# Two fused graph attention layers on one core: seeds of the next chunk of rows written before the chunk changes, and its conversions, row maxima and epilogue waits moved to later steps

## The chip, the core and the metric

The program runs on 1 core of a Trainium2 chip. The metric is the device time of one execution in microseconds (us). Three runs of the kernel before took 660.51, 660.71 and 661.35 us; their median is 660.71 us. The profiled execution took 661.77 us, of which the profile's span covers 660.0 us.

Engines in the profile: PE is TensorE (PEld its weight loads), DVE is VectorE, ACT is ScalarE, POOL is GpSimd, SP is SyncE, which here only issues DMAs.

## The reference

Two layers work on `x` (4096 nodes, 64 features) and one adjacency matrix `adj` (4096 x 4096, int32, symmetric, about 0.2% ones). Each is masked softmax attention, a residual and a layer norm:

```
Wh = item_embs @ W;  We = entity_embs @ W
scores = (Wh @ a1)[:, None] + (We @ a2)[None, :]
e = where(scores > 0, scores, 0.2 * scores);  e = where(adj > 0, e, NEG_BIG)
h = softmax(e, axis=1) @ entity_embs + item_embs
x = layernorm(x + elu(h))                       # layer 0
wh = x @ weight_w
e = leaky_relu((wh @ a_src)[:, None] + (wh @ a_dst)[None, :], 0.01)
x = layernorm(x + softmax(where(adj > 0, e, -1e9), axis=1) @ wh + bias)   # layer 1
```

## The kernel before, in words

**Chunks and steps.** The 4096 output rows are 32 row tiles of 128. They are worked through in chunks of 4, 8, 8, 8 and 4 tiles (`WIDTHS`), twice: chunks C0 to C4 are layer 0, C5 to C9 layer 1. A chunk goes through 32 steps J = 0..31, one for each tile of 128 columns of `adj`. The step number over the whole program is k = 32C + J, so C2 begins with step 64 and C7 with step 224. One step does this:

- PE multiplies the mask tile `v` with a diagonal matrix `D` of the chunk (L986) into one of three PSUM buffers `zps` (`ZB = 3`). This writes, or adds, the mask's term of the scores.
- The term of the leaky ReLU comes in one of two ways. In an unseeded step DVE adds it after the matmul (L816, `SCALAR_TENSOR_TENSOR`, for short the STT). In a seeded step ACT has written it ahead (L605, a Relu of `S_row`, the seed) and the matmul adds on top of it, so DVE has nothing to do.
- ACT takes the exponential into `Pm` (L613), in every step.
- PE multiplies `Pm` with the features (L941) and in layer 0 with ones (L948), two steps later (`LAG = 2`).

`SEEDS` says how many steps of each chunk are seeded. A seed of step n is issued on ACT one or two steps before n, ahead of the exponential of that step (`seeds_at`). It has to wait for its buffer: the user three places before it in the list `users` must be done. Before the change, only steps whose buffer was last used by a step of the same chunk may be seeded (`may`).

**What is done beside the steps.** While chunk C runs, the next chunk is prepared. In layer 0 the int32 `adj` halves of its tiles are converted to `v`: by DVE (L701, `compare`) or, for the tiles in `ACT_TILES` (4, 6, 8, 10, 20 and 24), by ACT (L506, `convert`). `halves_at` gives the step. C3 has the tiles 20 to 27, so the first tile that is converted during C2 is one of ACT's. In both layers DVE takes maxima over each row tile in two pieces (L722, `row_max`; `pieces_at` gives the step), which in layer 0 read the converted tile. At J = 30 DVE makes the next chunk's `D` (L733 to L744, `diagonals`). PE cannot begin the next chunk before that (`D_ready`).

**The epilogue of the chunk that ended** runs on POOL during the next chunk (L398 to L435), with parts elsewhere at fixed steps: ACT saves the sums at J = 1 (L543) and the projected rows at J = 4 (L560, L565), PE projects at J = 3 (L915, L920), DVE takes reciprocals at J = 7 (L441) and reduces `sums`, `squares` and (layer 0) `scores` at the steps of `AFTER_WIDE`, `AFTER_LAST` (C4) and `IN_LAYER_1`; in layer 0 the new row scores are turned on PE at J = `rows` and saved by ACT one step later (L516, L517).

**Order.** There is no scheduler: every engine executes its program in the order in which the loops over C and J write it, and waits on semaphores where named. Within a step DVE's order is: reductions of the epilogue, STT, conversions, row maxima, at J = 30 the diagonals. ACT's is: parts of the epilogue, conversions, seeds, exponential. On SP's queue a chunk's loads of `adj` come first, then the stores of the rows that ACT saved (L332, L334), then the load of `S_row` for the next chunk but one in the buffer of the same parity (L326).

## Time and profile before

| | |
|---|---|
| median of 3 runs | 660.71 us |
| profiled execution | 661.77 us |
| span of the profile | 660.0 us |
| DVE busy | 575.0 us, 87% of the span |
| ACT busy | 516.2 us, 78% |
| PE busy | 515.8 us, 78% |
| POOL busy | 191.6 us, 29% |
| TensorE clock granted, mean | 0.954 of 2.4 GHz |

A chunk is best read from the end of its `D` on DVE to the end of the next chunk's `D`, since between these two DVE does one chunk's whole work and PE runs one chunk's steps. The ends lie at 107.1, 179.9, 254.4 and 318.7 us (for C1 to C4) and at 390.5, 436.2, 496.3, 559.8 and 615.9 us (for C5 to C9). A busy share near the length of such a stretch says that the engine could not have done the chunk in much less. The gap between C4's last step and C5 (about 26 us) is the serial passage from layer 0 to layer 1.

### The profile page before, as it was taken

The numbers are of one execution on the slowest core, as the hardware profiler recorded it, in microseconds if no ns is written. First come the engines' busy times: TensorE is split into PE (matmuls) and PEld (weight loads), VectorE is DVE, ScalarE is ACT, GpSimd is POOL, SyncE is SP. The second block draws the span as 40 slices with busy tenths as digits, with TensorE's granted clock in tenths as the row PEclk, the third lists the DMA queues.
The fourth block names the chain that finished last, engine by engine and source line by source line (L and its number), as shares of the span: only waits on it lengthen the run. The fifth ranks groups of instructions, "written<-read, shape, count | busy, mean of one in ns | idle before, by whom it ended". The sixth has DMA issues, their size and how long they took to land.

```text
span 660.0 us, 14220 instructions
## 1 busy us (share of the span) xinstructions
PE 515.8 (78%) x6038; PEld 230.8 (35%) x6039; DVE 575.0 (87%) x729; ACT 516.2 (78%) x592; POOL 191.6 (29%) x143
## 2 busy tenths in 40 slices
PE   1304779899989799999988318778897898899894
PEld 1202345343443344444454203233333233333341
DVE  3888998999999898888467889989998998899685
ACT  0855998899999996898676227979997899699673
POOL 0110000388028850672083000004311450232240
PEclk9999889899999899999998758999999999999998
DMA  7899885687478727430200000000000001000000
GB/s 165 319 360 334 280 285 210 241 288 257 180 242 291 250 94 287 132 126 2 73 3 18 1 32 1 1 33 1 2 9 33 1 1 33 1 1 18 1 17 9
DMA packets 18631, 76.46 MB, mean 116 GB/s; under 512 B 6552, under 2 KB 8776, under 8 KB 10376
## 3 DMA queue, kind: packets, MB, share of 16 engines
q1 hardware_dynamic: 17560, 74.63, 32.5%
q8 instruction: 47, 0.77, 0.5%
q0 software_dynamic: 256, 0.80, 0.4%
...
HBM read 74.47 MB, written 1.09 MB: 114 GB/s over the span
## 4 chain that ended last, share of the span: by engine, by line
PE 31%; DVE 25%; ACT 20%; issue 14%; DMA 4%; POOL 3%; SPq 1%; POOLq 0%; ACTq 0%; DVEq 0%
PE acc L941 16%; ACT Pm L613 14%; DVE junk L722 12%; PE zps L986 9%; DVE zps L816 8%; PE acc L948 4%; DMA adj_in<-in_adj 4%; ACT zps L605 2%; ACT v L506 2%; SPq L350 1%; DVE v L701 1%; DVE tAB L697 1%; ACT u_row L522 1%; DVE tot L757 0%; DVE tot L753 0%
## 5 line engine op out<-in xcount | busy, mean ns | idle before, releaser
L613 ACT ACTIVATE Pm<-zps,ebias 128x1024 f32<-128x1024 f32 (+1 forms) x320 | 293.4, 933 | 82.6 <-DVE zps L816 68.3
L722 DVE CUSTOM_DVE_ANT_0 junk<-v,u_row 128x2048 int8<-128x2048 int8 (+3 forms) x136 | 304.6, 2261 | 2.0 <-ACT v L506 1.8
L986 PE MATMUL zps<-D,v 128*128 128x128 bf16 x2048 | 173.7, 224 | 56.1 <-DVE D L744 29.1
L986 PEld LDWEIGHTS zps<-D,v 128*128 128x128 fp8e4 x2048 | 118.7, 99 | 216.3 <-issue 87.3
L816 DVE SCALAR_TENSOR_TENSOR zps<-S_row,tau_col,zps 128x1024 f32<-128x1024 f32 (+1 forms) x136 | 142.0, 1050 | 50.6 <-PE zps L986 47.7
L605 ACT ACTIVATE zps<-S_row,ntau_col 128x1024 f32<-128x1024 f32 (+1 forms) x184 | 176.6, 960 | 5.4
L941 PE MATMUL acc<-Pm,X 128*32 128x512 f32 (+1 forms) x1280 | 145.5, 527 | 20.2 <-ACT Pm L613 17.8
L941 PE MATMUL acc<-Pm,VE 128*32 128x512 f32 (+1 forms) x1280 | 148.6, 538 | 8.5 <-ACT Pm L613 3.9
L398 POOL TENSOR_TENSOR tAB<-flag,totW 128x520 f32<-128x520 f32 (+1 forms) x8 | 10.3, 1287 | 282.5 <-issue 138.7
L948 PE MATMUL acc<-Pm,ones 128*32 128x256 f32 (+1 forms) x1280 | 87.8, 347 | 0.0
L948 PEld LDWEIGHTS acc<-Pm,ones 128*32 128x32 f32 x1280 | 43.1, 115 | 72.2 <-issue 62.7
L701 DVE TENSOR_SCALAR v<-adj_in 128x2048 fp8e4<-128x2048 int32 x44 | 62.7, 1428 | 1.0 <-DMA adj_in<-in_adj 1.0
L506 ACT ACTIVATE v<-adj_in,tanh_bias 128x2048 fp8e4<-128x2048 int32 x20 | 39.7, 2003 | 7.9 <-DMA adj_in<-in_adj 7.9
L941 PEld LDWEIGHTS acc<-Pm,X 128*32 128x32 f32 x1280 | 25.4, 108 | 42.4 <-ACT Pm L613 29.7
L941 PEld LDWEIGHTS acc<-Pm,VE 128*32 128x32 f32 x1280 | 25.8, 110 | 28.1 <-ACT Pm L613 11.6
L466 POOL TENSOR_SCALAR var<-tot 128x8 f32<-128x8 f32 (+1 forms) x10 | 7.7, 773 | 64.6 <-DVE tot L757 64.6
L405 POOL TENSOR_TENSOR o<-o,rden 128x512 f32<-128x512 f32 (+1 forms) x8 | 13.2, 1644 | 27.4 <-DVE rden L441 27.4
L401 POOL TENSOR_TENSOR o<-o,tAB 128x520 f32<-128x520 f32 (+1 forms) x8 | 13.5, 1687 | 25.8 <-ACT o L560 14.7
L467 POOL TENSOR_TENSOR rstd<-var,mhalf 128x8 f32<-128x8 f32 (+1 forms) x10 | 18.1, 1809 | 0.8
L887 PE MATMUL acc<-identf,ext 128*2 128x128 f32 (+2 forms) x3 | 1.1, 374 | 21.3 <-DVE ext L659 21.3
L506 ACT ACT_TABLE_LOAD x1 | 1.3, 1283 | 19.1 <-DMA adj_in<-in_adj 19.1
L425 POOL TENSOR_SCALAR mean<-tot 128x8 f32<-128x8 f32 (+1 forms) x8 | 6.4, 804 | 30.3 <-DVE tot L753 30.3
...
## 6 DMA issues: line engine op xcount, KB each, us to landing
...
```

Of the source, the lines that this page charges most:

```text
L401: ns.tensor_tensor(o[:, 0:n, :], o[:, 0:n, :], tA[:, 0:n, :], ALU.add).then_inc(flag_added, 1)
L405: link(ns.tensor_tensor(h, h, per_row(rden[:, 0:n]), ALU.mult))
L467: g.tensor_tensor(rstd[:, 0:R(C)], var[:, 0:R(C)], mhalf[:, 0:R(C)], ALU.pow).then_inc(rstd_done, 1)
L506: a.activation(v[:, H // 2, H % 2 * HALF:(H % 2 + 1) * HALF], adj_in[:, H % AB, :], ACT.Tanh, bias=tanh_bias[:, :], scale=40.0, saturate=F ...
L605: a.activation(zps[:, buf("step", n), 0:R(C) * P], S_row[:, C % 2, 0:R(C) * P], ACT.Relu, bias=ntau_col[:, n % JT:n % JT + 1]).then_inc(se ...
L613: a.activation(Pm[:, k % PB, 0:R(C) * P], zps[:, buf("step", k), 0:R(C) * P], ACT.Exp, bias=ebias[:, int(seeded(k)), J:J + 1])\
L701: d.tensor_scalar(v[:, H // 2, H % 2 * HALF:(H % 2 + 1) * HALF], adj_in[:, H % AB, :], 0.0, 0.5, ALU.is_gt, ALU.subtract, saturate=False). ...
L722: d.tensor_tensor_reduce(out=junk[:, at % 2, 0:cols.stop - cols.start], in0=v_bytes[:, rt, cols], in1=u_row[:, cols], scale=1.0, scalar=-3 ...
L816: d.scalar_tensor_tensor(z, S_row[:, C % 2, 0:R(C) * P], tau_col[:, J:J + 1], z, ALU.max, ALU.add).then_inc(z_done, 1)
L941: last = t.matmul(acc[s * F + f:s * F + f + G, 0, 0:w], V[:, f:f + G], Pm[:, k % PB, s * w:(s + 1) * w], start=first, stop=end)
L948: last = t.matmul(acc[q * G:(q + 1) * G, 1, 0:w], ones[:, :], Pm[:, k % PB, q * w:(q + 1) * w], start=first, stop=end)
L986: last = t.matmul(zps[:, buf("step", k), r * P:(r + 1) * P], v[:, chunks[C][1] + r, J * P:(J + 1) * P], D[:, C % 2, r, :], start=(r * P % ...
```

## The change

Four things change.

1. The rule of which steps may be seeded is widened: the buffer's last user may be a step of the chunk before, in the same layer, if that chunk is at least as wide. ACT then writes the seed for the next chunk at J = 30 and first waits until `S_row` of that chunk has landed (`wait_S`). The counts in `SEEDS` stay. Seeded steps per chunk were 28, 27, 27, 16, 12 and 28, 18, 18, 10, 0; they are 28, 27, 28, 16, 12 and the same in layer 1.
2. The seeded steps are spread by another formula, which takes the first candidate instead of the last. C2, C3, C4, C7 and C8 now begin with a seeded step 0; C1 and C6 begin with steps 0, 1 and 2 unseeded, as before. C0 and C5 keep their pattern.
3. `CLEAR = 3`: in every chunk except C0, the conversions for the next chunk begin at J = 3 instead of J = 0 and the row maxima at J = 4 instead of J = 1. Their last steps stay (25 and 28), so they stand closer.
4. The steps at which DVE, PE and ACT do their parts of POOL's epilogue are 1 to 2 later (`elu` 11 to 12, `sums` 14 to 16, `squares` 18 to 20, `scores` 24 to 26, `rows` 26 to 28; in layer 1 14 to 16 and 19 to 21). `AFTER_LAST` (C4) stays.

```diff
-    AFTER_WIDE = dict(elu=11, sums=14, squares=18, scores=24, rows=26)
+
+    CLEAR = 3
+    AFTER_WIDE = dict(elu=12, sums=16, squares=20, scores=26, rows=28)
     AFTER_LAST = dict(elu=10, sums=13, squares=17, scores=21, rows=22)
-    IN_LAYER_1 = dict(sums=14, squares=19)
+    IN_LAYER_1 = dict(sums=16, squares=21)
...
             may = [k for k in range(JT * C, JT * (C + 1)) if place["step", k] >= ZB
-                   and users[place["step", k] - ZB][0] == "step" and users[place["step", k] - ZB][1] >= JT * C]
+                   and users[place["step", k] - ZB][0] == "step"
+                   and users[place["step", k] - ZB][1] >= JT * FIRSTS[layer(C)]
+                   and R(users[place["step", k] - ZB][1] // JT) >= R(C)]
             n = SEEDS[layer(C)][C - FIRSTS[layer(C)]]
-            seeded_steps |= {k for i, k in enumerate(may) if (i + 1) * n // len(may) > i * n // len(may)}
+            seeded_steps |= {k for i, k in enumerate(may) if i * n % len(may) < n}
...
-            return [h for h in range(first, end) if (h - first) * 27 // (end - first) == J]
+            clear = CLEAR if C else 0
+            return [h for h in range(first, end) if clear + (h - first) * (27 - clear) // (end - first) == J]
...
-            return [(i, i // 2, i % 2) for i in range(n) if i * 29 // n + 1 == J]
+            clear = CLEAR if C else 0
+            return [(i, i // 2, i % 2) for i in range(n) if clear + i * (29 - clear) // n + 1 == J]
...
                     for n in seeds_at.get(k, []):
+                        of = n // JT
+                        if of > C:
+                            wait_S(act, of)
                         wait_buf(act, "step", n)
-                        a.activation(zps[:, buf("step", n), 0:R(C) * P], S_row[:, C % 2, 0:R(C) * P], ACT.Relu,
+                        a.activation(zps[:, buf("step", n), 0:R(of) * P], S_row[:, of % 2, 0:R(of) * P], ACT.Relu,
                                      bias=ntau_col[:, n % JT:n % JT + 1]).then_inc(seed_done, 1)
```

The lines move by 7 to 10 in the changed kernel (L816 is L826 there, L722 is L732, L613 is L623, L605 is L615, L506 is L513).

DVE at the start of C2, from the last operation of C1 on (`D` is C2's, the STTs are steps of C2, `junk,um` is a row maximum for C3). Before:

```order
L744 TENSOR_SCALAR D<-identb,g 128x128 x8
L816 SCALAR_TENSOR_TENSOR zps<-S_row,tau_col,zps 128x1024 x2
L722 ISA junk,um<-v,u_row 128x2048
L722 ISA um 128x1
L816 SCALAR_TENSOR_TENSOR zps<-S_row,tau_col,zps 128x1024
L722 ISA junk,um<-v,u_row 128x2048
```

and after the change:

```order
L754 TENSOR_SCALAR D<-identb,g 128x128 x8
L826 SCALAR_TENSOR_TENSOR zps<-S_row,tau_col,zps 128x1024
L732 ISA junk,um<-v,u_row 128x2048
L732 ISA um 128x1
L826 SCALAR_TENSOR_TENSOR zps<-S_row,tau_col,zps 128x1024
```

Before, the STTs are those of steps 64, 65 and 66 and the first row maximum belongs to J = 1. After, the STTs are those of steps 65 (J = 1) and 69 (J = 5) and the first row maximum belongs to J = 4.

ACT over the change from C1 to C2, from the saved rows of the epilogue (L517, after the change L524) or the last seeds of C1 to the second conversion for C3. Before:

```order
L605 ACTIVATE zps<-S_row,ntau_col 128x1024
L613 ACTIVATE Pm<-zps,ebias 128x1024 x3
L506 ACTIVATE v<-adj_in,tanh_bias 128x2048
L613 ACTIVATE Pm<-zps,ebias 128x1024
L543 ACTIVATE tAB<-acc 128x512
L548 ACTIVATE tAB<-acc 128x256
L506 ACTIVATE v<-adj_in,tanh_bias 128x2048
```

and after the change:

```order
L524 ACTIVATE rowsS<-zps 4x128
L615 ACTIVATE zps<-S_row,ntau_col 128x1024
L623 ACTIVATE Pm<-zps,ebias 128x1024
L615 ACTIVATE zps<-S_row,ntau_col 128x1024
L623 ACTIVATE Pm<-zps,ebias 128x1024 x2
L615 ACTIVATE zps<-S_row,ntau_col 128x1024
L623 ACTIVATE Pm<-zps,ebias 128x1024
L550 ACTIVATE tAB<-acc 128x512
L555 ACTIVATE tAB<-acc 128x256
L623 ACTIVATE Pm<-zps,ebias 128x1024
L615 ACTIVATE zps<-S_row,ntau_col 128x1024
L623 ACTIVATE Pm<-zps,ebias 128x1024
```

The row that follows the last one shown is the first conversion for C3 (L513). The second seed after the saved rows is that of step 64, the next one that of step 66. The conversion was the work ahead of the first exponential of C2 and now stands behind the third.

DVE at the start of C7. Before:

```order
L744 TENSOR_SCALAR D<-identb,g 128x128 x8
L816 SCALAR_TENSOR_TENSOR zps<-S_row,tau_col,zps 128x1024 x2
L722 ISA junk,um<-v,u_row 128x2048
L722 ISA um 128x1
L816 SCALAR_TENSOR_TENSOR zps<-S_row,tau_col,zps 128x1024
```

and after the change:

```order
L754 TENSOR_SCALAR D<-identb,g 128x128 x8
L826 SCALAR_TENSOR_TENSOR zps<-S_row,tau_col,zps 128x1024 x2
L732 ISA junk,um<-v,u_row 128x2048
L732 ISA um 128x1
L826 SCALAR_TENSOR_TENSOR zps<-S_row,tau_col,zps 128x1024
```

The rows read alike, but the first two STTs were those of steps 224 and 225 (J = 0 and 1) and are now those of steps 225 and 227 (J = 1 and 3).

## Rows read from the trace of the kernel before

**Rows 1.** Windows, `D` to `D`: length; PE, PEld, DVE, ACT, POOL busy; clock; DMA.

```profile
107.10:179.90 72.80, 67.00 (x808) 29.85 (x801) 69.33 (x76) 66.52 (x71) 34.02 (x17) 0.98 0.63 220
179.90:254.40 74.50, 67.67 (x786) 29.73 (x782) 70.37 (x71) 72.59 (x72) 41.43 (x17) 0.98 0.67 233
254.40:318.70 64.30, 63.59 (x769) 28.52 (x762) 54.71 (x58) 52.76 (x56) 27.91 (x17) 1.00 0.36 123
390.50:436.20 45.70, 32.79 (x363) 13.14 (x364) 44.61 (x53) 37.73 (x60) 0.00 (x0) 0.89 0.01 1
436.20:496.30 60.10, 51.54 (x528) 20.13 (x525) 56.87 (x64) 54.17 (x55) 15.01 (x11) 1.00 0.04 14
496.30:559.80 63.50, 53.71 (x524) 20.74 (x520) 59.79 (x65) 54.38 (x54) 18.59 (x11) 0.97 0.04 13
559.80:615.90 56.10, 51.55 (x524) 20.38 (x520) 49.11 (x53) 47.33 (x47) 14.21 (x11) 1.00 0.03 9
```

**Rows 2.** Page, part 5: the exponentials; busy, mean ns, idle before and releaser.

```profile
L613 ACT ACTIVATE Pm<-zps,ebias 128x1024 f32<-128x1024 f32 (+1 forms) x320 | 293.4, 933 | 82.6 <-DVE zps L816 68.3
```

**Rows 3.** Timeline, DVE, start of C2: start us, us, operation, idle before.

```profile
180.98 1.29 DVE L816 SCALAR_TENSOR_TENSOR zps<-S_row,tau_col,zps 128x1024 f32<-128x1024 f32 x1 [1.09 <-PE zps L986]
182.88 1.29 DVE L816 SCALAR_TENSOR_TENSOR zps<-S_row,tau_col,zps 128x1024 f32<-128x1024 f32 x1 [0.61 <-PE zps L986]
184.08 2.28 DVE L722 CUSTOM_DVE_ANT_0 junk<-v,u_row 128x2048 int8<-128x2048 int8 x1
```

**Rows 4.** Timeline, ACT, start of C2.

```profile
182.30 1.11 ACT L613 ACTIVATE Pm<-zps,ebias 128x1024 f32<-128x1024 f32 x1
184.33 0.60 ACT L543 ACTIVATE tAB<-acc 128x512 f32<-128x512 f32 x1 [0.92 <-PE acc L948]
...
185.09 2.00 ACT L506 ACTIVATE v<-adj_in,tanh_bias 128x2048 fp8e4<-128x2048 int32 x1
...
188.13 1.12 ACT L605 ACTIVATE zps<-S_row,ntau_col 128x1024 f32<-128x1024 f32 x1
```

**Rows 5.** Timeline, ACT and SP, saved rows and load of `S_row` in C1.

```profile
171.37 0.25 ACT L517 ACTIVATE rowsS<-zps 4x128 f32<-4x128 f32 x1
...
172.39 0.35 SPq L326 DMA_DIRECT2D S_row<-S_rows_scratch  x1
```

**Rows 6.** The landing of that load of `S_row` (L326).

```profile
DMA to landing us min/median/max: 5.2/5.2/5.2
```

**Rows 7.** Timeline, DVE, start of C7.

```profile
497.32 1.29 DVE L816 SCALAR_TENSOR_TENSOR zps<-S_row,tau_col,zps 128x1024 f32<-128x1024 f32 x1 [1.02 <-PE zps L986]
...
499.99 2.28 DVE L722 CUSTOM_DVE_ANT_0 junk<-v,u_row 128x2048 int8<-128x2048 int8 x1
```

**Rows 8.** Timeline, PE, start of C7: the projection and step 227.

```profile
501.46 1.16 PE L915 MATMUL zps<-W1p,tAB 128*128 128x130 f32 x8
502.46 0.61 PE L986 MATMUL zps<-D,v 128*128 128x128 bf16 x8
```

**Rows 9.** Timeline, DVE, start of C6.

```profile
440.33 2.29 DVE L722 CUSTOM_DVE_ANT_0 junk<-v,u_row 128x2048 int8<-128x2048 int8 x1
```

**Rows 10.** Timeline, ACT, start of C6: step 194.

```profile
443.86 1.11 ACT L613 ACTIVATE Pm<-zps,ebias 128x1024 f32<-128x1024 f32 x1 [2.07 <-DVE zps L816]
```

**Rows 11.** Timeline, DVE, start of C5.

```profile
392.65 3.79 DVE L697 TENSOR_REDUCE tAB<-X 128x64 f32<-128x2048 f32 x1
...
400.77 0.75 DVE L816 SCALAR_TENSOR_TENSOR zps<-S_row,tau_col,zps 128x512 f32<-128x512 f32 x1
```

**Rows 12.** Timeline, ACT, start of C8: steps 261 and 262.

```profile
574.74 2.12 ACT L613 ACTIVATE Pm<-zps,ebias 128x1024 f32<-128x1024 f32 x2 [2.79 <-DVE zps L816]
```

**Rows 13.** Groups by form, DVE, C2: row maxima, busy and mean ns.

```profile
L722 DVE CUSTOM_DVE_ANT_0 junk<-v,u_row 128x2048 int8<-128x2048 int8 x16 | 41.0, 2564 | 0.0
```

**Rows 14.** Timeline, POOL, C9: last operation of C8's epilogue.

```profile
639.26 1.04 POOL L430 TENSOR_TENSOR tAB<-tAB,rstd 128x512 f32<-128x512 f32 x1
```

**Rows 15.** Timeline, ACT, end of C9: the sums are saved.

```profile
649.93 0.38 ACT L543 ACTIVATE tAB<-acc 128x256 f32<-128x256 f32 x1 [0.76 <-PE acc L941]
```

## The prediction, made before the changed kernel ran

> **What bounds the kernel now.** I read the windows from the end of one `D` to the end of the next first. In five of the seven chunks shown DVE is busy for nearly the whole length: 69.33 of 72.80 us in C1, 70.37 of 74.50 in C2, 44.61 of 45.70 in C5, 56.87 of 60.10 in C6, 59.79 of 63.50 in C7 [rows 1]. So DVE idles 3.5, 4.1, 1.1, 3.2 and 3.7 us there, 15.6 us in all. ACT is as full in C2 (72.59 of 74.50) and has 6 to 9 us of idle time in C1, C5, C6 and C7. In C3 PE is the full one, 63.59 of 64.30 us. Only C8 leaves every engine room (PE 51.55, DVE 49.11, ACT 47.33 of 56.10). The page's groups then say that the exponentials are waited for: ACT sat idle 82.6 us ahead of them, 68.3 us of it until an STT of DVE came [rows 2]. That reads like a chance for this change, since many of these waits lie in a chunk's first steps. But an idle ACT beside a full DVE gives nothing back: to shorten such a chunk, DVE must do less or wait less. So the question for each part is what DVE does between one `D` and the next.
>
> **What the change does to DVE's work.** A seed takes one STT (1.29 us [rows 3]) from DVE and gives ACT a Relu (1.12 us [rows 4]). The counts stay, except that C2 gets one seed more. So DVE saves 1.3 us in the whole kernel, and seeds across the boundary only move the other STTs to later steps of the same chunk. The row maxima and conversions keep their number too, and so does POOL's epilogue. What changes is when DVE may do them. Because every engine runs in program order, the STTs of J = 0 to 3 now stand in front of the first row maximum, and DVE has nothing to put into the waits between them. `CLEAR` takes away the cover.
>
> **C2.** `D` ends at 179.9 us, which I call 0. Before, DVE waits 1.1 and 0.6 us, does two STTs and starts the first row maximum at 4.2 [rows 3]; 2.4 us of its idle time lies later. After, that first maximum reads tile 20, which ACT converts at J = 3. ACT gets there like this: the sums of C1 are saved at 4.4 as before (they wait for PE's last products of C1) and take 0.9 with the second copy; then exponential 65, seed 67, exponential 66 at 1.1 each and the conversion at 2.0 [rows 4]. That is 10.7 at the earliest. It can be later by the new wait for `S_row`: rows saved until 171.6, load issued at 172.4, landed 5.2 us behind that [rows 5, 6], so 6.0 us from saved to landed, of which ACT fills 2.2 with a seed and an exponential. The 3.8 us left are partly hidden, since DVE still has two maxima, an STT and `D` to do after the scores that this depends on (2 x 2.28 + 1.29 + 3.0 = 8.9 us), but exponentials 62, 63 and seed 66 then still stand ahead of exponential 64; worked through, that makes the first maximum up to 1.9 later, 12.6. I take 11.5. DVE does one STT until then, so it idles 10.2, and 1.5 more ahead of step 69, whose buffer waits for rows that ACT saves after that conversion. Of the 2.4 us of later idle time I leave 0.6, as the reductions come two steps later and wait less for POOL. Sum: 70.4 - 1.3 + 10.2 + 1.5 + 0.6 = 81.4 against 74.5: **+6.9 us**. Bounds: 10.7 and no other wait, +4.0; 12.6 with all waits, +9.8.
>
> **C7.** `D` ends at 496.3. DVE's first maximum now follows the STT of step 227. PE reaches that step only after the projection, 502.46 + 0.61 [rows 8], and nothing in the change makes the projection earlier, since it waits for the saved sums. So the STT runs from 6.8 to 8.1, and DVE has done two STTs, 2.5 us of work, by then. Before, it had idled 1.2 us by that time and done 6.9 [rows 7]. Loss 4.4. DVE's other idle time in C7 is 2.5 us, from STTs for which it came early; now it comes late, and I let 1.1 of it vanish: **+3.3** (bounds 1.9 and 4.4).
>
> **C6.** Steps 192 to 194 are unseeded before and after, then 196 is. Before, one row maximum lay between the second and third STT, from 440.33 [rows 9], and one more behind it. After, STT 194 ends at 441.6, exponential 194 at about 444.0 (two exponentials and a seed of 1.1 each behind 440.7; before it began at 443.86 [rows 10]), and step 196, which takes that buffer, has its STT until 446.5. By then DVE is two maxima behind and one STT ahead, 4.6 - 1.3 = 3.3. It can recover part of 1.4 us: **+2.5** (2.1 to 3.3).
>
> **C5.** DVE sums the columns until 396.4, then did two maxima and STT 164 at 400.77 [rows 11]. Now STT 164 comes first. PE was held by the column totals too and needs three small steps, ACT a copy, until about 399.0. DVE waits 2.6 us, and it was full otherwise: **+2.6** (1.8 to 3.1).
>
> **C1.** Three STTs run back to back, then a conversion; then STT 37 waits for saved rows: **+1.0** (-0.6 to 2.0).
>
> **C8.** Here DVE has 7.0 us idle, so a smoother start counts. Exponential 261 began at 574.74, 14.9 behind `D`, after a wait of 2.79 us [rows 12]. Without maxima between the STTs I get 12.0. That is 2.9 us, of which a maximum that is still to be done takes some: **-2.0** (-4.0 to 1.0).
>
> **At nothing.** C3: PE is full and idles 0.7 us [rows 1]; DVE's later start is hidden by its 9.6 idle us (-0.7 to 1.5). C0 keeps its order. C4 is tied to POOL's chain, whose steps stay. C9: C8's epilogue ends on POOL at 640.3 [rows 14]; two steps of 0.9 us later is 642.1, and ACT needs the stored result only at 649.93 [rows 15].
>
> **The sum.** 1.0 + 6.9 + 2.6 + 2.5 + 3.3 - 2.0 = 14.3 us on the execution profiled, 661.8 to 676.1; on the median of 660.7 that is **675.0 us**. The bounds add up to +4.5 and +25.1.
>
> **GpSimd's port.** Row maxima alone take 2.28 us [rows 3]; the 16 of C2, where POOL is busy 41.4 of 74.5 us, take 2.56 on the mean [rows 13, 1]. Of the maxima, two in each of C1, C2, C6 and C7 move from steps ahead of POOL's epilogue into it. At 0.28 each that is 2.2 us, which I leave to the range, as POOL meets DVE no longer than before. The Trainium skill (SBUF — State Buffer, "Who interferes with whom") says that a DVE instruction with two SBUF inputs and a GpSimd instruction exclude each other: the second fully blocks until the first is through. The trace's mean of 0.28 us is far from that for the maxima.
>
> **Rivals.**
> - *VectorE catches up* (668 us). The losses at the starts are real, but the idle time inside the chunks is used up by them in full, C2's first maximum comes at 10.7, C8 gives 4: about +7. For it: 2.5 us in C7 and 2.4 in C2 are there. Against it: C5 has none.
> - *The wait for `S_row` is in the open* (681 us). At each of three boundaries (C1 to C4) up to 3.8 us of ACT; half of that on top of the sum, +6. ACT is full in C2, which speaks for it; DVE's rest of 8.9 us against it.
> - *The maxima collide with GpSimd* (693 us). If each of the eight moved ones were held up by its own length, 8 x 2.28 = 18 us more. The mean in C2 speaks against it.
> - *Faster: the starts were the bound* (651 us). ACT waits behind row maxima at the starts (2.07 us in C6 [rows 10], 2.79 in C8 [rows 12]). If the STTs, free of them, came so soon that DVE waited under 1 us at a start, it would start its maxima no later than before and chunks could shrink by DVE's idle time, 15.6 us in five of them and some 5 in C8. Half of that is -10. It decides at the first maximum of C2: it would have to start before 5 us behind `D`. The conversion on ACT in front of it speaks against that.
> - *Nothing moves* (660.7 us): gains at C8 and C3 cancel the rest.
>
> **Numbers.** Forecast 0.50, catching up 0.22, `S_row` 0.10, GpSimd 0.04, faster 0.09, nothing 0.05. Within 0.2% (1.3 us) is what a measurement of this kernel cannot tell from no change. Slower by more than that 0.86, within it 0.05, faster 0.09. The range of 8 in 10 leaves out the faster case, nothing and the collision: 665 to 683 us.
>
> **What would show it.** Right: the windows of C2, C5, C6 and C7 are longer by 7, 3, 2.5 and 3 us with DVE's busy time unchanged; DVE's idle time sits ahead of the STTs and the first maximum of each chunk, and in C2 ends with ACT's conversion; ACT and PE wait for DVE late in the chunks. C3 stays at 64 us, C8 is shorter. Wrong: first maxima at 5 us behind `D` or sooner, or chunks whose DVE busy time fell by more than an STT.

## The result: 682.3 us, slower by 3.2%

The changed kernel takes 682.25 us (median of 4, 681.46 to 682.68) against 661.03 for the kernel before (median of 4): ratio 1.0315, 95% interval 1.0294 to 1.0337, so +21.2 us. The forecast was 675.0 in a range of 665 to 683. Sign and range hold, the range by less than 1 us, and the number is 7 us short. The execution profiled took 682.1 us, its span 680.3 (before: 661.8 and 660.0). The engines' busy times, part 1 of the page of the changed kernel:

```profile
PE 519.7 (76%) x6039; PEld 231.3 (34%) x6039; DVE 573.1 (84%) x728; ACT 518.3 (76%) x593; POOL 181.3 (27%) x143
```

In the kernel before DVE was busy 575.0 us, so it now works 1.9 us less while the span is 20.3 us longer. ACT is busy 2.1 us longer, 1.1 of it for one seed more, and PE 3.9 us longer with one matmul more on record (6039 for 6038). On DVE, the engine that the forecast watched, all of the loss is waiting. Part 5 of the page names the groups that wait (busy, mean ns of one, then idle time before the group and what ended most of it); first the kernel before, then the changed one:

```profile
L722 DVE CUSTOM_DVE_ANT_0 junk<-v,u_row 128x2048 int8<-128x2048 int8 (+3 forms) x136 | 304.6, 2261 | 2.0 <-ACT v L506 1.8
L816 DVE SCALAR_TENSOR_TENSOR zps<-S_row,tau_col,zps 128x1024 f32<-128x1024 f32 (+1 forms) x136 | 142.0, 1050 | 50.6 <-PE zps L986 47.7
```

```profile
L732 DVE CUSTOM_DVE_ANT_0 junk<-v,u_row 128x2048 int8<-128x2048 int8 (+3 forms) x136 | 305.2, 2269 | 8.0 <-ACT v L513 7.9
L826 DVE SCALAR_TENSOR_TENSOR zps<-S_row,tau_col,zps 128x1024 f32<-128x1024 f32 (+1 forms) x135 | 140.3, 1048 | 70.5 <-PE zps L996 67.7
```

DVE waits 70.5 us ahead of its STTs, up from 50.6, and 8.0 ahead of the row maxima, up from 2.0: 25.9 us more between them, on the engine that was full in five of the seven chunks of [rows 1]. Where it lies shows in the windows from `D` to `D` of the changed kernel, C1 to C3 and C5 to C8, columns as in [rows 1]:

```profile
107.90:184.00 76.10, 67.77 (x804) 29.99 (x796) 69.82 (x75) 67.26 (x71) 28.75 (x17) 0.96 0.60 211
184.00:265.70 81.70, 68.50 (x782) 29.70 (x782) 69.17 (x70) 73.84 (x74) 32.48 (x17) 0.98 0.61 213
265.70:333.20 67.50, 65.36 (x782) 29.17 (x782) 54.51 (x59) 51.83 (x55) 30.58 (x17) 1.00 0.33 110
403.20:452.90 49.70, 33.33 (x372) 13.29 (x372) 44.64 (x52) 39.26 (x62) 0.00 (x0) 0.90 0.04 12
452.90:515.90 63.00, 52.85 (x516) 20.61 (x516) 57.60 (x65) 54.78 (x54) 10.40 (x11) 0.97 0.03 11
515.90:578.90 63.00, 52.41 (x520) 20.37 (x520) 57.29 (x64) 54.96 (x54) 20.34 (x11) 1.00 0.03 10
578.90:635.60 56.70, 52.73 (x520) 20.75 (x520) 48.53 (x52) 44.72 (x44) 15.19 (x11) 0.97 0.02 6
```

Length less DVE's busy time is what it idles. In C2 that is 12.5 us, where it was 4.1, and in C1 6.3 (3.5), C3 13.0 (9.6), C5 5.1 (1.1), C6 5.4 (3.2), C7 5.7 (3.7), C8 8.2 (7.0).

Below stands every kernel that ran, by chunk: how much longer (us) each chunk is, from the end of one `D` to the end of the next, than in the profiled execution of the kernel before. "Median" is the difference of the medians of timed executions on one chip. The last column runs from C9's `D` to the end. The chunks come from one execution each. How far they scatter can be seen where a kernel's order in a chunk is that of the kernel before: C0 and what precedes it by about 1 us, C1 by up to 0.9 (only_spread, across_c7), C4 by up to 1.2 (more_seeds, across_c7), C2, C3 and C5 to C9 by 0.3 at most.

```
                median     C1    C2    C3    C4    C5    C6    C7    C8    C9
forecast         +14.3   +1.0  +6.9   0     0    +2.6  +2.5  +3.3  -2.0   0
after            +21.2   +3.4  +7.3  +3.1  -1.9  +4.2  +2.8  -0.5  +0.6  +0.6
no_clear         +11.8   +0.9  +2.6  +3.4  -1.9   0.0  +3.0  -1.3  +3.1  +0.6
only_clear       +13.2   +1.8  +5.9  -0.4  -0.2  +4.2  +1.7  -0.4  +1.3   0.0
clear_max        +16.7   +1.7  +5.3  +1.3  -1.2  +4.2  +1.6  -0.4  +1.2  -0.1
only_seeds        +5.7   -0.9  +0.8  +3.7  -2.1   0.0  +2.9  -1.5  +2.0  +0.6
only_across       +4.1    0.0  +0.9  +1.1   0.0   0.0  +0.7  -3.4  +4.2  -0.1
only_spread      +13.0   -0.9   0.0  +6.4  -0.8   0.0  +2.6  +0.5  +2.5  +0.6
only_late         +5.8   +0.7  +2.4  +1.9  -2.3   0.0  +2.0  -0.2  +0.7   0.0
late_rows         +4.5   +1.6  +2.4  +1.7  -2.3   0.0   0.0  -0.3   0.0  -0.1
d_first          +20.0   -0.1  +6.9  +4.2  +1.1  +4.2  +1.6  +0.7  -2.2  +1.9
tile21           +18.8   +2.9  +3.1  +4.2  -1.2  +4.2  +3.7  +0.2  +0.6  +0.6
more_seeds        +2.6   +0.2  -0.1   0.0  -1.2   0.0  +1.6  -1.7  +2.9   0.0
across_c7         -4.0   -0.8   0.0   0.0  -1.2   0.0   0.0  -3.4   0.0  -0.1
```

**The start of C2**, where the forecast had its largest term: DVE's timeline in the changed kernel, with `D` ending at 184.0.

```profile
186.73 1.29 DVE L826 SCALAR_TENSOR_TENSOR zps<-S_row,tau_col,zps 128x1024 f32<-128x1024 f32 x1 [2.77 <-PE zps L996]
194.09 2.29 DVE L732 CUSTOM_DVE_ANT_0 junk<-v,u_row 128x2048 int8<-128x2048 int8 x1 [6.07 <-ACT v L513]
...
197.76 1.29 DVE L826 SCALAR_TENSOR_TENSOR zps<-S_row,tau_col,zps 128x1024 f32<-128x1024 f32 x1 [1.37 <-PE zps L996]
```

One STT, then 6.07 us for a tile that ACT converts. The first row maximum starts 10.1 behind `D`; before it started at 4.2 [rows 3]. ACT's timeline there:

```profile
188.11 0.60 ACT L550 ACTIVATE tAB<-acc 128x512 f32<-128x512 f32 x1 [1.82 <-PE acc L958]
...
192.07 1.99 ACT L513 ACTIVATE v<-adj_in,tanh_bias 128x2048 fp8e4<-128x2048 int32 x1
```

The saving of the sums at 4.1 behind `D` and the conversion at 8.1 with 2.0 of its own are the steps that the forecast added up.

**The end of C1**, which the forecast did not have. PE's timeline of the changed kernel, J = 26 to 28:

```profile
172.89 0.37 PE L875 MATMUL zps<-identf,uS 128*4 128x128 f32 x1 [4.52 <-DVE uS L778]
...
174.26 1.94 PE L951 MATMUL acc<-Pm,VE 128*32 128x512 f32 x8
...
177.68 1.07 PE L951 MATMUL acc<-Pm,VE 128*32 128x512 f32 x8
```

And the same place in the kernel before, at its J = 24:

```profile
167.97 0.27 PE L865 MATMUL zps<-identf,uS 128*4 128x128 f32 x1 [0.47 <-DVE uS L768]
...
168.73 1.06 PE L941 MATMUL acc<-Pm,VE 128*32 128x512 f32 x8
```

PE turns the scores' rows, for which DVE makes `uS` out of sums over `tAB` (two reductions and two short operations). Before, `uS` was 0.47 us late. Now DVE is late, and PE stands still for 4.52 us, then works slowly: the products of a step take 1.94 us, not 1.07. This pause comes with `CLEAR`: PE's wait for `uS` in C1 is 4.40 us in only_clear, 4.38 in clear_max and 4.50 in tile21, and under 0.5 in no_clear, only_seeds and only_late (these kernels are described below). DVE has its maxima and conversions in fewer steps there and reaches the scores late. Windows of the changed kernel in that stretch and behind it (the clock is the third column from the end):

```profile
172.90:177.70 4.80, 4.80 (x37) 2.23 (x37) 4.35 (x4) 2.42 (x4) 0.00 (x0) 0.54 0.04 12
177.70:182.00 4.30, 4.30 (x53) 1.87 (x56) 2.09 (x6) 2.24 (x3) 0.00 (x0) 1.00 0.97 332
```

The granted clock is 0.54 of full, about the lower level (1.2 GHz), for 4.8 us right behind the pause, and full again after it. At the end of this chunk DVE, which caused the pause, has to wait for PE in its turn:

```profile
177.17 0.08 DVE L732 DVE_READ_ACCUMULATOR2_ANT um<- 128x1 f32 x1
179.77 1.29 DVE L826 SCALAR_TENSOR_TENSOR zps<-S_row,tau_col,zps 128x1024 f32<-128x1024 f32 x1 [2.52 <-PE zps L996]
...
182.56 1.39 DVE L754 TENSOR_SCALAR D<-identb,g 128x128 bf16<-128x128 bf16 x8
```

The row maxima are done at 177.2; `D` could be made, but STT 30 of the chunk stands in front of it in DVE's order and waits 2.52 us. This is how a delay of DVE was handed to PE and came back, with the slow clock on top. In C2 it is the same (PE idle 4.26 us, STT 30 waiting 2.05). The wait of STT 30 has a second condition: that step 30 is the one without a seed, right ahead of `D`, comes from the later rows (only_late below).

### The profile page after: what moved, and what is told of

It reads as the page before. It is cut to its first block, busy times and chain, and to the rows that moved or that the text cites. A ratio compares the mean times of both kernels' runs of the same rounds, so it can differ in the third digit from the quotient of the medians.

```text
span 680.3 us, 14226 instructions
## 1 busy us (share of the span) xinstructions
PE 519.7 (76%) x6039; PEld 231.3 (34%) x6039; DVE 573.1 (84%) x728; ACT 518.3 (76%) x593; POOL 181.3 (27%) x143
## 4 chain that ended last, share of the span: by engine, by line
DVE 48%; PE 25%; issue 11%; ACT 8%; DMA 5%; POOL 2%; SPq 1%; POOLq 0%; ACTq 0%; DVEq 0%
DVE junk L732 27%; PE acc L951 13%; DVE zps L826 10%; PE zps L996 8%; DMA adj_in<-in_adj 4%; ACT Pm L623 4%; DVE v L711 3%; PE acc L958 3%; ACT v L513 2%; DVE D L754 1%; ACT zps L615 1%; DVE tot L767 1%; DVE tAB L707 1%; DVE tot L763 1%; SPq L357 1%
## 5 line engine op out<-in xcount | busy, mean ns | idle before, releaser
L623 ACT ACTIVATE Pm<-zps,ebias 128x1024 f32<-128x1024 f32 (+1 forms) x320 | 293.9, 934 | 87.9 <-DVE zps L826 68.1
L732 DVE CUSTOM_DVE_ANT_0 junk<-v,u_row 128x2048 int8<-128x2048 int8 (+3 forms) x136 | 305.2, 2269 | 8.0 <-ACT v L513 7.9
L826 DVE SCALAR_TENSOR_TENSOR zps<-S_row,tau_col,zps 128x1024 f32<-128x1024 f32 (+1 forms) x135 | 140.3, 1048 | 70.5 <-PE zps L996 67.7
L615 ACT ACTIVATE zps<-S_row,ntau_col 128x1024 f32<-128x1024 f32 (+1 forms) x185 | 177.8, 961 | 11.0 <-DMA S_row<-S_rows_scratch 5.3
L405 POOL TENSOR_TENSOR tAB<-flag,totW 128x520 f32<-128x520 f32 (+1 forms) x8 | 8.2, 1025 | 281.6 <-issue 137.8
L513 ACT ACTIVATE v<-adj_in,tanh_bias 128x2048 fp8e4<-128x2048 int32 x20 | 39.7, 2004 | 8.8 <-DMA adj_in<-in_adj 8.8
L412 POOL TENSOR_TENSOR o<-o,rden 128x512 f32<-128x512 f32 (+1 forms) x8 | 13.2, 1648 | 25.7 <-DVE rden L448 25.7
L432 POOL TENSOR_SCALAR mean<-tot 128x8 f32<-128x8 f32 (+1 forms) x8 | 2.5, 312 | 58.7 <-DVE tot L763 58.7
L474 POOL TENSOR_TENSOR rstd<-var,mhalf 128x8 f32<-128x8 f32 (+1 forms) x10 | 16.3, 1629 | 0.8
L408 POOL TENSOR_TENSOR o<-o,tAB 128x520 f32<-128x520 f32 (+1 forms) x8 | 11.1, 1385 | 16.8 <-ACT o L574 9.0
```

Of the source, the lines that this page charges most:

```text
L408: ns.tensor_tensor(o[:, 0:n, :], o[:, 0:n, :], tA[:, 0:n, :], ALU.add).then_inc(flag_added, 1)
L412: link(ns.tensor_tensor(h, h, per_row(rden[:, 0:n]), ALU.mult))
L474: g.tensor_tensor(rstd[:, 0:R(C)], var[:, 0:R(C)], mhalf[:, 0:R(C)], ALU.pow).then_inc(rstd_done, 1)
L513: a.activation(v[:, H // 2, H % 2 * HALF:(H % 2 + 1) * HALF], adj_in[:, H % AB, :], ACT.Tanh, bias=tanh_bias[:, :], scale=40.0, saturate=F ...
L615: a.activation(zps[:, buf("step", n), 0:R(of) * P], S_row[:, of % 2, 0:R(of) * P], ACT.Relu, bias=ntau_col[:, n % JT:n % JT + 1]).then_inc ...
L623: a.activation(Pm[:, k % PB, 0:R(C) * P], zps[:, buf("step", k), 0:R(C) * P], ACT.Exp, bias=ebias[:, int(seeded(k)), J:J + 1])\
```

## The experiments

The theories, by the letters in the expectations. **A**, cover: `CLEAR` takes row maxima and conversions away from the first steps, so that DVE has nothing to do in the waits there. **B**: ACT's new wait for `S_row` is in the open. **C**: the scores two steps later make PE wait, and the next chunk's rows come late. **D**: `D` stands behind step 30's STT, and the time lost there is the price.

**no_clear** and **only_clear**: `CLEAR` away from the change, and `CLEAR` alone on the kernel before.

```
-    CLEAR = 3
+    CLEAR = 0
```

```
+    CLEAR = 3
-            return [h for h in range(first, end) if (h - first) * 27 // (end - first) == J]
+            clear = CLEAR if C else 0
+            return [h for h in range(first, end) if clear + (h - first) * (27 - clear) // (end - first) == J]
-            return [(i, i // 2, i % 2) for i in range(n) if i * 29 // n + 1 == J]
+            return [(i, i // 2, i % 2) for i in range(n) if clear + i * (29 - clear) // n + 1 == J]
```

> The changed kernel (682.3 us) with CLEAR = 0: conversions and row maxima start at J = 0 and 1 again, seeds across the boundary and later epilogue steps stay. Theory A (taking the row maxima and conversions out of steps 0 to 3 removes DVE's cover): C2, C5, C6 lose most of their extra 7.3, 4.1 and 2.8 us, and C1's late part too, since DVE reaches the scores of J = 26 sooner; 664 us (660 to 668). Theory B (ACT's wait for S_row at J = 30 and the rows saved one step before it are the cost): at least 674 us. Theory C (the epilogue's later steps make PE wait at J = 28 for the scores): 670 to 676 us.

> The kernel before (661.0 us) with CLEAR = 3 alone; seeds and epilogue steps as before. Theory A: most of the loss, 674 to 680 us, with DVE waiting 6 us and more ahead of the first row maximum of C2. Theory B and C: under 668 us, since neither the wait for S_row nor the later scores are there.

Measured: no_clear 673.63 us (ratio 1.0183, 1.0140 to 1.0227), only_clear 675.07 (1.0203, 1.0170 to 1.0236). `CLEAR` alone costs 13.2 us, and 9.5 where it comes on top of the rest (21.2 - 11.8). With it come C2's +5.9 and C5's +4.2, and without it they are +2.6 and 0.0. This speaks for A in those two chunks, and only_clear lies where A had it (674 to 680), though DVE waits only 4.17 us ahead of C2's first maximum there, not 6. But no_clear is outside A's 660 to 668 and inside C's 670 to 676. It is still 11.8 us slower than before, and nearly all of the forecast's sum was `CLEAR`'s. So the other parts, costed at almost nothing, lose nearly as much.

**only_seeds** and **only_late**: each of the other two parts alone on the kernel before.

```
-                   and users[place["step", k] - ZB][0] == "step" and users[place["step", k] - ZB][1] >= JT * C]
+                   and users[place["step", k] - ZB][0] == "step"
+                   and users[place["step", k] - ZB][1] >= JT * FIRSTS[layer(C)]
+                   and R(users[place["step", k] - ZB][1] // JT) >= R(C)]
-            seeded_steps |= {k for i, k in enumerate(may) if (i + 1) * n // len(may) > i * n // len(may)}
+            seeded_steps |= {k for i, k in enumerate(may) if i * n % len(may) < n}
```

```
-    AFTER_WIDE = dict(elu=11, sums=14, squares=18, scores=24, rows=26)
+    AFTER_WIDE = dict(elu=12, sums=16, squares=20, scores=26, rows=28)
-    IN_LAYER_1 = dict(sums=14, squares=19)
+    IN_LAYER_1 = dict(sums=16, squares=21)
```

> The kernel before with the new rule and spread of the seeds alone (CLEAR = 0, epilogue steps as before). Theory A: the first steps have their row maxima beside them, the rows are saved at J = 27, three steps ahead of the first seed for the next chunk, so S_row has landed: 657 to 662 us. Theory B: 665 us or more.

> The kernel before with the later epilogue steps alone (sums 16, squares 20, scores 26, rows 28; 16 and 21 in layer 1). Theory A: DVE's waits for POOL in C2 (2.0 us) go, PE may wait at J = 28: 659 to 663 us. Theory C: 666 us or more, with PE idle over 3 us ahead of the rows' transposition in C1 and C2 and TensorE's clock at the lower level behind it.

Measured: only_seeds 667.52 (1.0086, 1.0053 to 1.0119), +5.7 us; only_late 667.68 (1.0092, 1.0056 to 1.0128), +5.8. The three parts add up to 13.2 + 5.7 + 5.8 = 24.7 us against 21.2 for all of them, and these two to 11.5 against the 11.8 of no_clear. In their sum they are nearly independent; chunk by chunk they are not (C3 +3.7 and +1.9 alone, +3.4 together).

Both kernels reach the number of the theory that they were to test, and neither by its mechanism. In only_seeds ACT waits nowhere for `S_row`: the rows are saved at J = 27 and have landed by J = 30. So B isn't the cause of its 5.7 us; most of it lies in C3, C6 and C8 (+3.7, +2.9 and +2.0). In only_late PE doesn't wait for `uS` in C1 and C2 at all, where C wanted over 3 us. The pause is `CLEAR`'s, as shown above. In only_late the loss has two places; ACT's timeline at the start of C2 has one, DVE's at the end of C1 the other:

```profile
182.38 2.00 ACT L506 ACTIVATE v<-adj_in,tanh_bias 128x2048 fp8e4<-128x2048 int32 x1 [3.07 <-DMA adj_in<-in_adj]
```

```profile
175.86 1.29 DVE L816 SCALAR_TENSOR_TENSOR zps<-S_row,tau_col,zps 128x1024 f32<-128x1024 f32 x1 [1.67 <-PE zps L986]
```

The second is STT 30 ahead of `D`. It is there because the saved rows take their buffer at J = 28 instead of 26, and the step that may have no seed moves with them, to step 30. The first is a load of `adj_in` that comes late. SP's queue tells why:

```profile
175.26 0.35 SPq L326 DMA_DIRECT2D S_row<-S_rows_scratch  x1
175.66 9.08 SPq L319 DMA_DIRECT2D adj_in<-in_adj  x4
```

The loads stand behind the store of the rows and the load of `S_row`, both two steps later now (the load of `S_row` went out at 172.39 in the kernel before [rows 5]). The forecast took the epilogue's steps for GpSimd's and ACT's business; they are also SP's.

**d_first**: in the changed kernel `D` is made a step sooner, ahead of STT 30.

```
-                    if J == JT - 2 and nxt < NCH and nxt != NC:
+                    if J == JT - 3 and nxt < NCH and nxt != NC:
```

> The changed kernel (682.3 us) with the next chunk's D made by DVE at J = 29 instead of J = 30, so ahead of the STT of step 30, which the change left unseeded in C1, C2, C3, C6, C7 and C8. Theory D (part of the loss is that D now stands behind an STT that waits for PE; DVE sat idle 2.5 and 2.1 us there in C1 and C2): D comes 1 to 2.5 us sooner in six chunks, 672 to 677 us. Theory A alone (only the cover of steps 0 to 3): within 2 us of 682.

Measured: 680.54 us (1.0295, 1.0274 to 1.0317), 1.7 below the changed kernel by the medians (1.2 by the column of differences), with intervals that overlap. That is the 680 to 684 of A alone, not the 672 to 677 of D. `D` does come sooner, C1 is 3.5 us shorter than in the changed kernel; DVE's timeline of d_first shows what becomes of it:

```profile
178.67 1.39 DVE L754 TENSOR_SCALAR D<-identb,g 128x128 bf16<-128x128 bf16 x8
179.97 1.28 DVE L826 SCALAR_TENSOR_TENSOR zps<-S_row,tau_col,zps 128x1024 f32<-128x1024 f32 x1
185.68 1.29 DVE L826 SCALAR_TENSOR_TENSOR zps<-S_row,tau_col,zps 128x1024 f32<-128x1024 f32 x1 [4.43 <-PE zps L996]
```

DVE meets a wait of 4.43 us behind `D` in place of the 2.52 in front of it and the 2.77 behind, and PE still turns the rows at 172.68 after 4.51 us of idle time. But C3, C4, C7 and C9 are 1.1, 3.0, 1.2 and 1.3 us longer than in the changed kernel, and C8 2.8 shorter. So STT 30 is a place where the delay shows, but moving `D` ahead of it wins almost nothing: PE's pause lies further up and is still there.

**tile21**: in the changed kernel ACT converts tiles 21 and 25 where it did 20 and 24, so that the first row maxima of C2 read a tile that DVE converted itself.

```
-    BY_ACT = (slice(0, 4), slice(4, 12, 2), slice(20, 28, 4))
+    BY_ACT = (slice(0, 4), slice(4, 12, 2), slice(21, 28, 4))
```

> The changed kernel with ACT converting the tiles 21 and 25 instead of 20 and 24, so that DVE converts the first tile of C3 itself. In C2 DVE then need not sit 6.1 us ahead of its first row maximum until ACT's conversion at J = 3. Theory A with the step as predicted (the first maximum is held by that conversion): C2 shorter by 3 to 5 us, 677 to 679 us. If DVE was held by the STTs of the first steps rather than by the conversion: under 1.5 us.

Measured: 679.39 us (1.0273, 1.0245 to 1.0301), 2.9 below the changed kernel by the medians and 2.4 by the differences, with intervals that overlap. C2 is 4.2 us shorter (+3.1 against +7.3). DVE's timeline, with `D` ending at 183.4:

```profile
187.36 2.36 DVE L711 TENSOR_SCALAR v<-adj_in 128x2048 fp8e4<-128x2048 int32 x2
189.63 2.28 DVE L732 CUSTOM_DVE_ANT_0 junk<-v,u_row 128x2048 int8<-128x2048 int8 x1
```

The first maximum stands at 6.2 behind `D` instead of 10.1. So the 6.07 us of waiting for `v` in C2 were ACT's conversion, and most of them were on the path. PE's pause ahead of `uS` in C2 (4.26 us in the changed kernel) is gone with them, which belongs to the 4.2. C3 and C6 are 2.0 us longer than in the changed kernel.

**only_spread** and **only_across**: the two halves of the seeds' part apart, the new spread with the old rule on boundaries, and seeds across boundaries with the old spread. The edit of the first is the last two lines of only_seeds' diff, that of the second all the other lines, with ACT's wait for `S_row` as in the change.

> The kernel before (about 661.5 us) with the new formula that spreads the seeds alone; no seeds across the boundary. Both seed edits together cost 5.7 us. Theory D: the spread makes step 30 unseeded instead of 29 in C3, C6, C7 and C8, which alone carries the loss: 665 to 667 us. Theory B (the wait for S_row at the boundary): 660 to 662 us.

> The kernel before with seeds allowed across the boundary alone, spread by the old formula, which leaves step 0 unseeded and seeds step 1. Theory D: step 30 stays seeded as before, so no loss: 658 to 662 us. Theory B: 664 us or more, with ACT idle until S_row has landed at J = 31.

Measured: only_spread 673.60 (1.0202, 1.0173 to 1.0232), only_across 664.64 (1.0062, 1.0040 to 1.0084). The new spread alone costs 13.0 us, more than both halves together (5.7). Half of it is in C3, and there the chain can be read. The timelines of only_spread at steps 24 and after, for ACT, PE and DVE:

```profile
309.07 1.11 ACT L613 ACTIVATE Pm<-zps,ebias 128x1024 f32<-128x1024 f32 x1 [2.88 <-DVE zps L816]
```

```profile
311.39 1.03 PE L986 MATMUL zps<-D,v 128*128 128x128 bf16 x8 [2.75 <-ACT zps L605]
```

```profile
315.41 1.29 DVE L816 SCALAR_TENSOR_TENSOR zps<-S_row,tau_col,zps 128x1024 f32<-128x1024 f32 x1 [4.17 <-PE zps L986]
```

A step without a seed now falls on J = 24, where DVE also makes the scores. ACT waits 2.88 us for that STT, PE waits 2.75 for ACT, DVE then waits 4.17 for PE, and the window behind PE's pause has the slow clock:

```profile
311.40:315.40 4.00, 4.00 (x36) 1.90 (x40) 0.00 (x0) 3.38 (x5) 0.00 (x0) 0.63 0.02 5
```

With seeds across the boundary the count of steps that may have one changes: in only_seeds steps 23 and 25 of C3 have no seed and 24 has one. That fits the two halves not adding up, but no kernel moved step 24 alone. Where the few unseeded steps stand matters more than how evenly they are spread. Theory D's forecasts failed in both kernels, 673.6 for 665 to 667 and 664.6 for 658 to 662 (its text has step 30 unseeded in C8 too; there it is 29 and 31). And only_across reaches B's 664 without B's mechanism, for ACT waits nowhere for `S_row` in it. What it shows beside that: C7 3.4 us shorter, C8 4.2 longer.

**late_rows** and **clear_max**: late_rows is the kernel before with the scores and rows alone two steps later; clear_max has `CLEAR` for the row maxima and leaves the conversions where they were.

```
-    AFTER_WIDE = dict(elu=11, sums=14, squares=18, scores=24, rows=26)
+    AFTER_WIDE = dict(elu=11, sums=14, squares=18, scores=26, rows=28)
```

```
+    CLEAR = 3
-            return [(i, i // 2, i % 2) for i in range(n) if i * 29 // n + 1 == J]
+            clear = CLEAR if C else 0
+            return [(i, i // 2, i % 2) for i in range(n) if clear + i * (29 - clear) // n + 1 == J]
```

> The kernel before with only the scores (step 26) and the rows (step 28) of layer 0 later; elu, sums and squares as before. All later steps together cost 6 us, with ACT idle 3.1 us ahead of the first conversion in C2, for an adj load that stands behind the saved rows on SP's queue, and DVE idle 1.7 to 2.1 us ahead of step 30's STT. If these two are the cost: C1, C2 and C3 with C4 as in that run, 664 to 667 us. If instead the later sums and squares cost it: under 662.5 us.

> The kernel before with only the row maxima from J = 4; the conversions start at J = 0 as before. CLEAR as a whole cost 13.5 us. Theory A (DVE has nothing beside the first STTs): C5 again +4.2 us, C6 and C8 +1 to 2; C2 less than its 5.9, since ACT converts tile 20 at J = 0 and the first maximum can start with its step: 668 to 672 us. If the conversions carry it: under 665 us.

Measured: late_rows 666.15 (1.0073, 1.0053 to 1.0093), clear_max 678.37 (1.0245, 1.0224 to 1.0267). The scores and rows carry 4.5 of only_late's 5.8 us, all in C1 to C4; what is left is C6's +2.0, from the sums and squares of layer 1. Clear_max is no faster than only_clear, and well above the 668 to 672 that was expected of it. By the medians it is 3.5 us slower, with intervals that just touch; the execution profiled was its fastest (675.7, the others 677.9 to 679.0), so the chunks don't show where that lies. For `CLEAR`'s loss it is enough to move the maxima. With the conversions in their old place, the first maximum of C2 comes sooner, and it gains nothing. DVE's timeline of clear_max, then of only_clear, both with `D` ending near 181.7:

```profile
189.42 2.28 DVE L724 CUSTOM_DVE_ANT_0 junk<-v,u_row 128x2048 int8<-128x2048 int8 x1
...
196.35 1.29 DVE L818 SCALAR_TENSOR_TENSOR zps<-S_row,tau_col,zps 128x1024 f32<-128x1024 f32 x1 [4.64 <-PE zps L988]
```

```profile
192.62 2.29 DVE L725 CUSTOM_DVE_ANT_0 junk<-v,u_row 128x2048 int8<-128x2048 int8 x1 [4.17 <-ACT v L509]
...
196.29 1.29 DVE L819 SCALAR_TENSOR_TENSOR zps<-S_row,tau_col,zps 128x1024 f32<-128x1024 f32 x1 [1.37 <-PE zps L989]
```

The maximum starts 3.2 us sooner, and STT 69 at the same time to 0.1 us: the wait goes from 4.17 + 1.37 to 4.64 in one piece. A second chain lay beside the first and ends as late. STT 69 needs PE's step 69, which follows ACT's exponentials and saved rows, and on ACT the conversion stands ahead of these in both kernels. The rows that free the buffer of step 69 are saved until 195.3 in both.

**more_seeds** and **across_c7**: two tries for a kernel that is faster than before. The first gives layer 1 six more seeds, so that DVE has less to do. The second is the kernel before with the wait for `S_row` and seeds across the boundary into C7 alone, where only_across had gained 3.4 us:

```
-SEEDS = ((29, 28, 28, 16, 12), (28, 18, 18, 10, 0))
+SEEDS = ((29, 28, 28, 16, 12), (28, 20, 20, 12, 0))
```

```
-                   and users[place["step", k] - ZB][0] == "step" and users[place["step", k] - ZB][1] >= JT * C]
+                   and users[place["step", k] - ZB][0] == "step"
+                   and users[place["step", k] - ZB][1] >= JT * (C - (C == 7))
+                   and R(users[place["step", k] - ZB][1] // JT) >= R(C)]
```

> The kernel before with more seeds in layer 1: 20, 20 and 12 in C6, C7 and C8 instead of 18, 18 and 10. If DVE's own work bounds C6 and C7 as the prediction had it, two STTs less (2.5 us) make each shorter by 1 to 2.5 us, ACT having 6 to 9 us free: 656 to 659 us. If the place of the unseeded steps matters as much as their number: anything from 658 to 664 us.

> The kernel before with seeds across the boundary into C7 alone, spread by the old formula. With seeds across everywhere C7 was 3.5 us shorter and C8 4.2 us longer. If the two are independent: 657 to 658.5 us. If C8's loss only follows from C7's gain: no change, 660 to 662 us.

Measured: more_seeds 664.24 (1.0034, 1.0020 to 1.0048), across_c7 **657.66 us** (0.9948, 0.9929 to 0.9967), the one kernel here that is faster than both, and where it was expected if C7 and C8 are independent. The windows of more_seeds for C6, C7 and C8:

```profile
432.90:494.50 61.60, 51.81 (x528) 20.11 (x525) 55.22 (x62) 56.10 (x57) 12.95 (x11) 1.00 0.04 15
494.50:556.30 61.80, 52.74 (x528) 20.39 (x520) 57.52 (x63) 56.40 (x56) 22.81 (x11) 1.00 0.04 12
556.30:615.30 59.00, 52.05 (x528) 20.40 (x520) 47.01 (x51) 49.06 (x49) 16.23 (x11) 1.00 0.03 8
```

(The execution profiled took 661.17 us, 3.1 below the median of 12; its chunks are read for their proportions.) In C6 DVE's work falls by 1.7 us, from 56.9 to 55.2, as intended, and its idle time grows from 3.2 to 6.4. In C7 the work falls by 2.3 and the chunk is 1.7 us shorter, as forecast. In C8 the work falls by 2.1 and the idle time grows from 7.0 to 12.0. Less work for the full engine is a gain in one of three chunks; in the other two more waiting took it back. And the window of C7 in across_c7:

```profile
494.60:554.70 60.10, 52.57 (x524) 20.37 (x520) 57.45 (x65) 54.63 (x54) 19.51 (x11) 1.00 0.05 14
```

Of the 3.4 us gained against [rows 1], 2.3 are DVE's busy time (59.8 to 57.5) and 1.1 its idle time. The busy time is the row maxima, by the groups of DVE in that chunk, the kernel before first, then across_c7, then the changed kernel:

```profile
L722 DVE CUSTOM_DVE_ANT_0 junk<-v,u_row 128x2048 int8<-128x2048 int8 x16 | 39.5, 2483 | 0.0
```

```profile
L732 DVE CUSTOM_DVE_ANT_0 junk<-v,u_row 128x2048 int8<-128x2048 int8 x16 | 37.4, 2346 | 0.0
```

```profile
L732 DVE CUSTOM_DVE_ANT_0 junk<-v,u_row 128x2048 int8<-128x2048 int8 x16 | 37.2, 2343 | 0.0
```

The same 16 instructions take 2.1 to 2.3 us less in both. One alone takes 2.28, so 16 take 36.5 undisturbed, and the kernel before paid 3.0 on top of that where these pay under 1. Which ones pay can be read by laying the timelines of DVE and POOL over each other, here in the kernel before:

```profile
518.04 3.28 DVE L722 CUSTOM_DVE_ANT_0 junk<-v,u_row 128x2048 int8<-128x2048 int8 x1
521.26 3.35 DVE L722 CUSTOM_DVE_ANT_0 junk<-v,u_row 128x2048 int8<-128x2048 int8 x1
```

```profile
517.90 1.28 POOL L408 TENSOR_TENSOR tAB<-o,X 128x512 f32<-128x512 f32 x1
519.26 3.21 POOL L421 TENSOR_TENSOR tAB<-tAB,bias_bc 128x512 f32<-128x512 f32 x1
```

The first maximum starts when POOL's L408 has 1.14 us left, and takes 1.00 us more than alone. POOL's L421 starts when that maximum has about 2.07 us left, and takes 3.21 us where it takes 1.28 alone (in C8). The second maximum starts when L421 has 1.20 us left, and takes 1.07 more. Every maximum of C7 that takes over 2.33 us starts inside a `TENSOR_TENSOR` of POOL and pays what is left of it, less 0.13 us: left 0.43, 1.14, 1.20, 0.19 and 0.97 us in the kernel before, paid 0.30, 1.00, 1.07, 0.06 and 0.84; left 0.56 and 0.74 in across_c7, paid 0.43 and 0.61; left 0.98 and 0.31 in the changed kernel, paid 0.85 and 0.17. POOL's small `TENSOR_TENSOR` (L467, 8 elements a partition) holds up none: a maximum that starts with 0.67 us of it left takes 2.28. So C7 got cheaper because fewer maxima started inside one of POOL's large instructions.

## Why the prediction was right in sign and 7 us short

- **The mechanism: right for `CLEAR`, absent for the rest.** DVE was the engine to watch, its work stayed, and its waits grew, by 25.9 us ahead of STTs and maxima. The faster rival needed the first maximum of C2 before 5 us behind `D`; it came at 10.1.
- **C2, +6.9: +7.3.** The working of the start held: first maximum at 10.1 (taken 11.5, earliest 10.7, so 0.6 under the bound), 1.37 us ahead of STT 69 (taken 1.5). What it had not seen is that the two waits lie in parallel (clear_max), and that the time the start saved against the forecast is spent at the chunk's end, where PE idles 4.26 us and STT 30 waits 2.05. That the sum came so near is in part luck. Only_clear has +5.9, so the other parts add 1.4 on top of it.
- **C6, +2.5: +2.8.** The size is right, but not by the start alone. Only_clear gives 1.7, no_clear gives 3.0: either is enough, and together they cost no more.
- **C1, +1.0: +3.4. The step that failed is "three STTs run back to back, then a conversion".** It looked at the chunk's start only. At its end `uS` is late, PE stops for 4.52 us, the clock is 0.54, and `D` waits behind STT 30 for 2.52 us. Single parts give -0.9 (seeds), +0.7 (late) and +1.8 (`CLEAR`), together 1.6. Against 3.4 that leaves 1.8, more than C1's scatter of 0.9, though four such numbers go into it: `CLEAR` alone has PE's pause but not the unseeded step 30 ahead of `D`, only_late has that step but no pause, and the change has both. This is read from the traces; no run tried these two together without the seeds' part.
- **C5, +2.6: +4.2, all of it `CLEAR`'s** (only_clear +4.2, no_clear 0.0). The wait for STT 164 was taken as 2.6 us and is 4.04:

```profile
413.10 0.76 DVE L826 SCALAR_TENSOR_TENSOR zps<-S_row,tau_col,zps 128x512 f32<-128x512 f32 x1 [4.04 <-PE zps L996]
```

  PE "needs three small steps" left out the clock. PE's products take 1.08 us each in two of these steps, where 0.64 is usual, which is some 0.9 of the 1.4 us that were missing. PE comes out of a pause of 4.86 us for the column totals, and the clock was at 0.50 already before that, from the start of C5 on (403.2 to 409.1 us). The windows of this stretch, the changed kernel's and then the one before's:

```profile
409.10:413.10 4.00, 3.99 (x34) 1.84 (x38) 0.00 (x1) 2.22 (x4) 0.00 (x0) 0.53 0.00 0
```

```profile
396.50:400.60 4.10, 4.10 (x34) 1.88 (x38) 4.10 (x3) 2.22 (x4) 0.00 (x0) 0.50 0.00 0
```

  The slow clock was there before too, 0.50, and it cost nothing, since DVE had 4.10 us of row maxima to do beside it; now it has 0.00. The trace of before held this row, and it was not read.
- **C7, +3.3: -0.5. The largest miss of one term.** The start came as worked out: STT 227 at 6.6 behind `D` (taken 6.8), and the first maximum behind it. DVE's idle time in the chunk grew by 2.0 (taken 3.3), within the bounds. But "with DVE's busy time unchanged" failed here: the maxima took 2.3 us less, since two of them and not five were held up by an instruction of POOL. Where they start follows from the whole order, and no term of the sum had it. Only_clear has -0.4 as well, with maxima of 2446 ns on the mean, so neither the seeds nor cheaper maxima are all of it.
- **C8, -2.0: +0.6.** The smoother start was to be worth 2.9 us. Exponential 261 does come sooner, 13.2 us behind `D` where it was 14.9 (taken 12.0), so the start gave 1.7. But the chunk ends no sooner, and DVE idles 8.2 us instead of 7.0. By no_clear (+3.1) and only_clear (+1.3) each part makes this chunk longer.
- **"At nothing": C3, C4 and C9, +0.6 to +1.2.** C3 +3.1 and C4 -1.9 belong together: `D` of C4 stands behind an STT of step 30 that had a seed before, so the border moves. The net is 1.2, and C4 alone scatters by as much. C9 is +0.6.
- **The parts costed at nothing** are the real failure. The forecast took the seeds as an STT saved and other STTs moved, and the epilogue's two steps as POOL's, and gave neither a loss of its own. They measured +5.7 and +5.8 us. What the sum was about is `CLEAR`, and there its 14.3 stands near the 13.2 of only_clear; but C7 (3.7 us less) and C8 (3.3 more) miss in opposite directions in that kernel too, so that this is part working and part luck. That 682.3 lies in the range is luck too: no term and no bound of the sum stood for the 11.5 us of the two other parts.
- **The port.** The forecast took the mean of 0.28 us per maximum as a sign against a full block. The mean hides it: most maxima pay nothing, and those that start inside a large instruction of POOL pay what is left of it, less 0.13 us, up to 1.07 us in C7. So the rule of the Trainium skill (SBUF — State Buffer, "Who interferes with whom"), that the second fully blocks until the first is through, is borne out by these traces for POOL's large instructions, on both engines (3.28 us for 2.28 on DVE, 3.21 for 1.28 on POOL). What failed in the collision rival (693 us) is its price: a maximum isn't held up by its own 2.28 us but by the rest of POOL's instruction, and all the maxima together took 305.2 us against 304.6 before.
- **`S_row` in the open, 681 us,** came closest in number, and not by its mechanism. ACT does wait for it, at the end of C1:

```profile
180.87 1.12 ACT L615 ACTIVATE zps<-S_row,ntau_col 128x1024 f32<-128x1024 f32 x1 [1.97 <-DMA S_row<-S_rows_scratch]
```

  That is 1.97 us, 1.65 at the end of C2 and 1.72 at the end of C3, 5.3 in all. In no_clear it is 2.96, 3.23 and 1.73 us. In only_seeds and only_across ACT doesn't wait for `S_row` at all, so the wait is there only where the seeds across the boundary meet the later rows. That meeting costs little: no_clear is 11.8 us slower, and the two parts alone add up to 11.5, with intervals of about 3 us either way. So the wait looks nearly hidden, as the forecast had it; no run removed it alone.

**Open.** How the seeds' part comes to +3.7 in C3 and +2.9 in C6; why C8 costs 4.2 us in only_across and 0.0 in across_c7, where the seeds of C8 are as before; whether the gain of across_c7 can be had together with a smoother start of C2, which was not tried.
